# VectorE weights the expert activation and GpSimd makes the low part of the gated rows, in a DiT block's mixture of experts

## The chip, the cores and the metric
The kernel runs on one core of one Trainium2 chip. The metric is the device time of one execution in microseconds (us), given as the median of several runs. The engines are TensorE (PE, matmul), VectorE (DVE), ScalarE (ACT), GpSimd (POOL) and SyncE (SP, which issues most DMAs).

## The reference
The input is 16 batches of 512 rows of 128 numbers. Each batch goes through a modulated layer norm and routed linear attention, then through a second norm, a small gated layer and a mixture of experts. The part that matters here is the last one:

```python
g = _silu(jnp.einsum('td,edh->eth', xt, exp_w1))     # 8 experts
u = jnp.einsum('td,edh->eth', xt, exp_w3)
yexp = jnp.einsum('eth,ehd->etd', g * u, exp_w2)
routed = jnp.einsum('te,etd->td', combine, yexp)     # combine: the router's weights
shared = _silu(xt @ sh_w1) * (xt @ sh_w3) @ sh_w2    # two more "experts" of weight 1
```

The kernel puts the router's weight ahead of the last product: it multiplies the activation `g` by it, so that the ten products with `w2` can be summed in one PSUM bank.

## The kernel before
The program has three stages. In the first, all 16 batches are normalised and routed. The second runs the attention over 160 blocks. The third runs the experts over 160 units, one for each batch b and expert n (`k = 10*b + n`; n is 0 to 7 for the routed experts, and 8 and 9 for the two shared ones). Work that belongs to the batches and not to the loops (gather of the attended rows, projection, second norm, small gated layer, router) is cut into steps, the "post" jobs. `post_pool`, `post_act`, `post_pe`, `post_freed` and `post_dve` put each step into a fixed slot of the second and third loops, one batch every 10 slots. The last gather lies at unit 64 of the expert stage and the last router step at about unit 103, so the last 56 units have no such work.

Every engine runs its own instruction list in order, and the engines meet at semaphores. No scheduler changes the order: it is the order of the code. For one unit k the work is:

- PE, `up(k)`: three matmuls for the gate (bank 1 or 2) and three for the up part (one of three banks in `wide`). The operands are split into a high and a low part, so each product takes three passes (L1630).
- ACT: silu of the gate product into `eg` (named `kvw` in the trace, L1686).
- POOL: for n below 8, `eg` times the weight rows that a DMA has spread in `hq` (L1595).
- DVE: up part times `eg` into `ep` (also `kvw`, L1724).
- ACT: the high part of `ep`, a copy that rounds to the matmul's type, into `epp` (L1691).
- DVE: the low part, `ep` minus the high part (L1717).
- PE, `down(k)`: three matmuls with `w2`, summed over the batch in bank 0 (L1640). It is issued three units after `up(k)`.

`eg`, `ep` and `epp` are rings of three buffers. In its turn k, DVE runs freed and tail work, then the low part of unit k-1, then the product of unit k, then `post_dve`. ACT runs the tail, silu of unit k, the high part of unit k-1, then `post_act`. PE runs `up(k)`, `post_pe`, the tail of the batch before, then `down(k-3)`. POOL runs the weighting of unit k, a gather step in eight of ten units while gathers last (n = 7, 8, 9, 0 to 4, L898), and at n = 3 `hidden_parts`, which splits the rows of the batch after the next into high and low (L1547, L1549). The tail is the last gated layer: `ys`, the copy of bank 0 (L1672), two products (L1647, L1650), a transposition (L1654), and the vector and scalar steps between (L1701, L1678, L1707).

Post steps named below: L1048 to L1056 and L1140 (DVE, an inverse root in many tiny operations, at n = 1, 2, 3), L930 (ACT, the normalised rows, at n = 4), L957 (PE, transpositions, among others of L930's rows at n = 5 and of the gathered rows at n = 6), L909 (ACT, weights the gathered rows, at n = 5 and 6, and waits for the gathers), L936 (ACT, at n = 5, behind L909; the transposition at n = 6 waits for it), L1011 (PE, at n = 4, waits for the router's last step L1100 on DVE, once in four batches).

Of the kernel before, what the change touches and what calls it, by code (L numbers as in the profile page):

```python
# [5 lines left out]
ALU = mybir.AluOpType  # L6
# [8 lines left out]
P = 128  # L15
# [5 lines left out]
E = 8  # L21
# [31 lines left out]
def adaln_block(nc, x, gate_wT, q_w, k_w, v_wT, fmT, norm_c, o_wT, lin0, lin0_b, s1w1, s1b1, s1w2, s1b2, fgateT,  # L53
                ew1, ew3, ew2, shw1, shw3, shw2, lin1, lin1_b, s2w1, s2b1, s2w2, s2b2, cT, wmod, out):
    ctx = ExitStack()
    with ctx:
# [3 lines left out]
        def sem(name):  # L60
            return ctx.enter_context(nc.semaphore(name))
# [825 lines left out]
        def post_pool(pool, slot):  # L887
            for k in range(NT * TOPA):
                b = at(k - GATHER, slot)
                if b is not None:  # L890
                    u, s = b % 2, sum(b >= x for x in B0[1:])
                    if k == 0:
                        for i in range(2):
                            pool.wait_ge(s_os[i], 16 * ((C0[s + 1] // 2 + 1 - i) // 2))
                        if b >= 2:
                            pool.wait_ge(s_onT, b - 1)
                    t = b * NT + k // TOPA
                    pool.indirect_dma_start(gst[:, u, k, :], None, orow[s],  # L898
                                            bass.IndirectOffsetOnAxis(idxs[:, t, k % TOPA:k % TOPA + 1], 0),
                                            bounds_check=BLOCKS[s] * P - 1, oob_is_err=False).then_inc(s_g[u], 16)  # L900
# [258 lines left out]
        s_cb = [sem("weight_rows_loaded0"), sem("weight_rows_loaded1")]  # L1159

        def rows_of(u, lo, hi):
            return hq[:, (u * E + lo) * NT:(u * E + hi) * NT, 0:D]
# [10 lines left out]
        def tb(name, shape, dt=F32):  # L1173
            return ph.enter_context(nc.sbuf_tensor(name, shape, dt))
# [368 lines left out]
        def hidden_parts(pool, b, u):  # L1543
            pool.wait_ge(s_h2, b + 1)
            h = h_all[:, b * NT:(b + 1) * NT, :]
            high, low = (hp[:, u, k, :].rearrange("p (i d) -> p i d", d=D) for k in range(2))
            pool.tensor_copy(high, h)  # L1547
            pool.drain()  # L1548
            pool.tensor_tensor(low, h, high, ALU.subtract).then_inc(s_hl, 1)  # L1549

        RING = 3
        eg, ep = (kvw[:, i * RING * S:(i + 1) * RING * S].rearrange("p (r t) -> p r t", t=S) for i in range(2))
        epp = tb("epp", [P, RING, 2, S], F32R)
# [6 lines left out]
        UNITS = NB * NU  # L1560
# [6 lines left out]
        s_es = sem("expert_gate")  # L1567
        s_eu = sem("expert_gate_weighted")
        s_ep = sem("expert_hidden")
        s_eh = sem("expert_hidden_high")  # L1570
        s_el = sem("expert_hidden_low")
# [11 lines left out]
        with nc.Block() as block:  # L1583
            @block.gpsimd
            def _(pool):
                for b in range(2):
                    hidden_parts(pool, b, b)
                for k in range(UNITS):
                    b, n = divmod(k, NU)
                    if n < E:  # L1590
                        if n == 0:
                            pool.wait_ge(s_cb[b % 2], 16 * (b // 2 + 1))
                        pool.wait_ge(s_es, k + 1)
                        g = eg[:, k % RING, :].rearrange("p (i t) -> p i t", t=P)
                        pool.tensor_tensor(g, g, rows_of(b % 2, n, n + 1), ALU.mult).then_inc(s_eu, 1)  # L1595
                    post_pool(pool, NBK + k)
                    if n == 3 and 0 < b < NB - 1:
                        pool.wait_ge(s_eg, NU * b)
                        hidden_parts(pool, b + 1, (b + 1) % 2)
# [95 lines left out]
            @block.vector  # L1695
            def _(dve):
                def tail(b, n):
                    if n == T3 + 1:
                        dve.wait_ge(s_t3, b + 1)
                        dve.wait_ge(s_t2c, b + 1)  # L1700
                        dve.scalar_tensor_tensor(out=t2[:, :], in0=bank[7][:, :], scalar=bias[:, 5:6], in1=tg[:, :],  # L1701
                                                 op0=ALU.add, op1=ALU.mult).then_inc(s_t3c, 1)
                    elif n == T4 + 1:
                        dve.wait_ge(s_t5, b + 1)
                        if b >= 2:
                            dve.wait_ge(s_out[b % 2], 16 * (b // 2))
                        dve.tensor_tensor(fin[:, b % 2, :, :], bank[7][:, :].rearrange("p (i d) -> p i d", d=D),  # L1707
                                          x_all[:, b * NT:(b + 1) * NT, :], ALU.add).then_inc(s_fin, 1)

                for k in range(UNITS + NU):  # L1710
                    b, n = divmod(k, NU)
                    post_freed(dve, NBK + k)
                    if b:
                        tail(b - 1, n)
                    if 1 <= k <= UNITS:
                        dve.wait_ge(s_eh, k)
                        dve.tensor_tensor(epp[:, (k - 1) % RING, 1, :], ep[:, (k - 1) % RING, :],  # L1717
                                          epp[:, (k - 1) % RING, 0, :], ALU.subtract).then_inc(s_el, 1)
                    if b < NB:
                        if n < E:  # L1720
                            dve.wait_ge(s_eu, E * b + n + 1)
                        else:
                            dve.wait_ge(s_es, k + 1)
                        dve.tensor_tensor(ep[:, k % RING, :], up_bank[k % RING][:, :], eg[:, k % RING, :],  # L1724
                                          ALU.mult).then_inc(s_ep, 1)
                    post_dve(dve, NBK + k)
# [35 lines left out]
```

## Time and profile before
| | |
|---|---|
| median of 3 runs | 1312.92 us (1306.09 to 1319.36) |
| the profiled execution | 1298.82 us |
| its span, first to last instruction | 1297.1 us |
| PE, DVE, ACT, POOL busy | 84%, 72%, 52%, 38% |
| mean granted TensorE clock | 0.941 |

The span is split by the three stages: the expert stage has its first matmul at 769.5 us and its last work at 1294 us. A share of busy time averages over stages with different limits. The clock is a share of 2.4 GHz: 1.00 is 2.4 GHz, 0.50 is 1.2 GHz, and a value between says that both occurred.

### The profile page before, as it was taken

What the parts mean: (1) busy time and instruction counts of PE and PEld (TensorE: products, weight loads), DVE (VectorE), ACT (ScalarE), POOL (GpSimd) and SP (SyncE); (2) the same over time, 40 slices, a digit from 0 to 9 for tenths busy, and PEclk for the clock granted to TensorE, in tenths of its full rate; (3) what the DMA queues carried; (4) which work ended last, traced back from release to release, by engine and by line L of the source; (5) the groups of instructions that cost most, each with busy time, mean ns of one, the idle gap of its engine ahead of it and who ended that gap; (6) DMA issues with size and microseconds to landing.
All of it is one profiled execution on the core that took longest, in us unless ns stands there. A gap on an engine that the chain in (4) does not pass through costs nothing. (4 is left out here: it accounts for less than half of the span.)

```text
span 1297.1 us, 26776 instructions
## 1 busy us (share of the span) xinstructions
PE 1090.8 (84%) x9288; PEld 787.8 (61%) x9288; DVE 934.8 (72%) x2058; ACT 668.4 (52%) x1645; POOL 491.8 (38%) x450
## 2 busy tenths in 40 slices
PE   4875589999999887899988977778886799889996
PEld 3554456676676555566656645556664566667774
DVE  4774568788876665777778748787778887776664
ACT  2542245555555545556666535645555555445553
POOL 2057023313323544322211226656655433455542
PEclk8986689999999999999999989889888899999999
DMA  9962123323333333222222134123322023233220
GB/s 310 372 255 89 45 83 99 111 76 104 111 104 91 101 93 89 77 66 64 63 62 57 49 108 123 31 69 92 88 87 86 19 85 90 66 95 98 74 81 17
DMA packets 83586, 125.76 MB, mean 97 GB/s; under 512 B 9088, under 2 KB 65920, under 8 KB 79360
## 3 DMA queue, kind: packets, MB, share of 16 engines
q1 hardware_dynamic: 73216, 98.86, 25.0%
q0 software_dynamic: 10240, 25.18, 6.2%
q8 instruction: 79, 1.29, 0.4%
q14 instruction: 51, 0.42, 0.1%
HBM read 71.32 MB, written 52.69 MB: 96 GB/s over the span
## 5 line engine op out<-in xcount | busy, mean ns | idle before, releaser
L1486 DVE SCALAR_TENSOR_TENSOR att<-reach,endrel,wide 128x1024 f32<-128x1024 f32 x160 | 204.8, 1280 | 87.1 <-PE wide L1398 68.8
L1595 POOL TENSOR_TENSOR kvw<-kvw,hq 128x512 f32<-128x512 f32 x128 | 170.4, 1333 | 227.0 <-ACT kvw L1686 220.9
L898 POOL DMA_INDIRECT gst<-attended_rows,idxs x128 | 139.0, 1086 | 254.0 <-DVE att L1486 129.1
L1717 DVE TENSOR_TENSOR epp<-kvw,epp 128x512 fp32r<-128x512 f32 x160 | 153.8, 961 | 104.2 <-ACT epp L1691 102.1
L252 POOL DMA_INDIRECT routed_rows<-hq,idxs x128 | 132.0, 1031 | 224.6 <-DVE att L1486 150.3
L1640 PE MATMUL bank<-epp,w2p 128*128 128x512 f32 x480 | 172.2, 469 | 9.6 <-DVE epp L1717 9.4
L1686 ACT ACTIVATE kvw<-bank 128x512 f32<-128x512 f32 x160 | 94.5, 591 | 111.0 <-PE wide L1630 110.8
L1630 PE MATMUL bank<-hp,w1p 128*128 128x512 f32 x480 | 144.2, 410 | 5.7 <-POOL hp L1549 4.7
L1691 ACT ACTIVATE epp<-kvw 128x512 fp32r<-128x512 f32 x160 | 100.4, 628 | 92.3 <-DVE kvw L1724 92.1
L1373 PE MATMUL bank<-kvw,turned 128*128 x320 | 142.9, 529 | 5.5 <-ACT turned L1283 1.6
L1630 PE MATMUL wide<-hp,w3p 128*128 128x512 f32 x480 | 142.2, 406 | 0.0
L1640 PEld LDWEIGHTS bank<-epp,w2p 128*128 128x128 f32 x480 | 90.2, 197 | 54.9 <-issue 27.3
L1290 ACT ACTIVATE k1s<-bank 128x128 f32<-128x128 f32 x160 | 44.2, 276 | 150.5 <-PE bank L1373 142.5
L1398 PE MATMUL wide<-turned,kx 32*128 32x128 f32 x2560 | 117.7, 298 | 0.9 <-DVE att L1486 0.7
L1724 DVE TENSOR_TENSOR kvw<-wide,kvw 128x512 f32<-128x512 f32 x160 | 109.0, 681 | 10.4 <-POOL kvw L1595 10.4
L1630 PEld LDWEIGHTS bank<-hp,w1p 128*128 128x128 f32 x480 | 94.3, 197 | 31.0 <-POOL hp L1549 5.6
L1630 PEld LDWEIGHTS wide<-hp,w3p 128*128 128x128 f32 x480 | 93.3, 194 | 22.9
L1443 PE MATMUL bank<-att,vx 128*32 128x128 f32 x2560 | 103.9, 280 | 0.0
L1398 PEld LDWEIGHTS wide<-turned,kx 32*128 32x128 f32 x2560 | 87.3, 187 | 20.9 <-issue 2.4
L1479 DVE TENSOR_TENSOR hq<-bank,k1s 128x128 f32<-128x128 f32 x160 | 46.3, 289 | 47.6 <-ACT vx L1293 38.9
L1318 ACT ACTIVATE oTs<-bank 128x256 f32<-128x256 f32 x80 | 30.5, 381 | 95.1 <-PE bank L1443 63.5
L1435 PE MATMUL bank<-hq 128*128 128x128 f32 x320 | 66.2, 289 | 9.4 <-DVE sh L1496 9.1
(265 smaller groups left out, 1914.3 us busy)
## 6 DMA issues: line engine op xcount, KB each, us to landing
hq<-weight_rows SPq DMA_DIRECT2D x16, 2048.0 KB
routed_rows<-zero SPq DMA_DIRECT2D x4, 5120.0 KB, 24.5
rows<-routed_rows SPq DMA_DIRECT2D x80, 256.0 KB
attended_rows<-ob SPq DMA_DIRECT2D x80, 128.0 KB
out<-fin SPq DMA_DIRECT2D x16, 256.0 KB
routed_rows<-hq,idxs POOLq DMA_INDIRECT x128
gst<-attended_rows,idxs POOLq DMA_INDIRECT x128
hq<-in_ew SPq DMA_DIRECT2D x3, 512.0 KB, 6.7
```

The costliest lines, as they stand in the source:

```text
L252: pool.indirect_dma_start(hs[s], bass.IndirectOffsetOnAxis(idxs[:, t, k:k + 1], 0), hq[:, t, :], None, bounds_check=BLOCKS[s] * P - 1, oob ...
L898: pool.indirect_dma_start(gst[:, u, k, :], None, orow[s], bass.IndirectOffsetOnAxis(idxs[:, t, k % TOPA:k % TOPA + 1], 0), bounds_check=BL ...
L1373: pe.matmul(bank[1][:, 0:KV], turned[:, n // 2 % 3, 0, n % 2, :], kvw[:, bass.ds(w, KV)], start=True, stop=True).then_inc(s_kv, 1)
L1398: mm = pe.matmul(wide[:, p, par * P:(par + 1) * P], kx[r, n // 2 % 2, par, a * P:(a + 1) * P], turned[r, n // 2 % 3, 1, a, :], start=True, ...
L1443: mm = pe.matmul(bank[2][32 * p:32 * p + 32, n % 2 * P:(n % 2 + 1) * P], v[:, (4 * p + par) * DK:(4 * p + par + 2) * DK], att[:, n % 2, p, ...
L1486: dve.scalar_tensor_tensor(out=att[:, n % 2, :, :], in0=reach[:, :, :].rearrange("p a c -> p (a c)").unsqueeze(1) .to_broadcast([P, 4, 2 * ...
L1595: pool.tensor_tensor(g, g, rows_of(b % 2, n, n + 1), ALU.mult).then_inc(s_eu, 1)
L1630: mm = pe.matmul(ps[:, :], w[:, wk, n, :], hp[:, b % 2, hk, :], start=(wk + hk == 0), stop=(hk == 1))
L1640: mm = pe.matmul(bank[0][:, :], w2p[:, wk, n, :], epp[:, k % RING, hk, :], start=(n + wk + hk == 0), stop=(n == NU - 1 and hk == 1))
L1691: act.activation(epp[:, (k - 1) % RING, 0, :], ep[:, (k - 1) % RING, :], ACT.Copy).then_inc(s_eh, 1)
L1717: dve.tensor_tensor(epp[:, (k - 1) % RING, 1, :], ep[:, (k - 1) % RING, :], epp[:, (k - 1) % RING, 0, :], ALU.subtract).then_inc(s_el, 1)
L1724: dve.tensor_tensor(ep[:, k % RING, :], up_bank[k % RING][:, :], eg[:, k % RING, :], ALU.mult).then_inc(s_ep, 1)
```

## The change
The two SBUF operations of a unit change engines. The weighting of the activation goes from POOL to DVE, right ahead of the product with the up part. The low part goes from DVE to POOL. POOL's loop gets one more turn, since it now works on unit k-1. DVE's product gets a wait for the low part of unit k-3, because `ep` is now read by another engine than the one that writes it.

```diff
@@ gpsimd
-                for k in range(UNITS):
+                for k in range(UNITS + 1):
                     b, n = divmod(k, NU)
-                    if n < E:
-                        if n == 0:
-                            pool.wait_ge(s_cb[b % 2], 16 * (b // 2 + 1))
-                        pool.wait_ge(s_es, k + 1)
-                        g = eg[:, k % RING, :].rearrange("p (i t) -> p i t", t=P)
-                        pool.tensor_tensor(g, g, rows_of(b % 2, n, n + 1), ALU.mult).then_inc(s_eu, 1)
+                    if k:
+                        pool.wait_ge(s_eh, k)
+                        pool.tensor_tensor(epp[:, (k - 1) % RING, 1, :], ep[:, (k - 1) % RING, :],
+                                           epp[:, (k - 1) % RING, 0, :], ALU.subtract).then_inc(s_el, 1)
                     post_pool(pool, NBK + k)
@@ vector
                     if b:
                         tail(b - 1, n)
-                    if 1 <= k <= UNITS:
-                        dve.wait_ge(s_eh, k)
-                        dve.tensor_tensor(epp[:, (k - 1) % RING, 1, :], ep[:, (k - 1) % RING, :],
-                                          epp[:, (k - 1) % RING, 0, :], ALU.subtract).then_inc(s_el, 1)
                     if b < NB:
+                        dve.wait_ge(s_es, k + 1)
+                        if n == 0:
+                            dve.wait_ge(s_cb[b % 2], 16 * (b // 2 + 1))
                         if n < E:
+                            g = eg[:, k % RING, :].rearrange("p (i t) -> p i t", t=P)
+                            dve.tensor_tensor(g, g, rows_of(b % 2, n, n + 1), ALU.mult).then_inc(s_eu, 1)
                             dve.wait_ge(s_eu, E * b + n + 1)
-                        else:
-                            dve.wait_ge(s_es, k + 1)
+                        if k >= RING:
+                            dve.wait_ge(s_el, k - RING + 1)
                         dve.tensor_tensor(ep[:, k % RING, :], up_bank[k % RING][:, :], eg[:, k % RING, :],
                                           ALU.mult).then_inc(s_ep, 1)
```

The lines of the later part move up by one or two: the low part is L1592 (POOL), the weighting L1719 and the product L1723 (DVE).

VectorE, units 2 and 3 of the first batch, before; `expert_hidden_high` is ACT's rounded copy, `expert_gate_weighted` POOL's weighting, `deviation_chain` orders the tiny operations:

```order
L1053 SCALAR_TENSOR_TENSOR tmp<-tmp,var 128x36 [waits deviation_chain]
L1717 TENSOR_TENSOR epp<-kvw,epp 128x512 [waits expert_hidden_high,deviation_chain]
L1724 TENSOR_TENSOR kvw<-wide,kvw 128x512 [waits expert_gate_weighted]
L1056 SCALAR_TENSOR_TENSOR inv<-tmp,inv 128x36
L1051 TENSOR_TENSOR tmp<-inv 128x36 [waits deviation_chain]
```

The same place after the change; `expert_gate` is ACT's silu:

```order
L1053 SCALAR_TENSOR_TENSOR tmp<-tmp,var 128x36 [waits deviation_chain]
L1719 TENSOR_TENSOR kvw<-kvw,hq 128x512 [waits expert_gate,deviation_chain]
L1723 TENSOR_TENSOR kvw<-wide,kvw 128x512 [waits expert_gate_weighted]
L1056 SCALAR_TENSOR_TENSOR inv<-tmp,inv 128x36
L1051 TENSOR_TENSOR tmp<-inv 128x36 [waits deviation_chain]
```

The low part L1717, which waited for ACT's copy of the unit before, has left this list. Its place is taken by the weighting L1719, which waits for this unit's silu.

GpSimd, around `hidden_parts` of a batch with gathers, before (the three rows ahead of the cast are n = 2 and 3, the last two are n = 4):

```order
L898 DMA gst<-attended_rows3,idxs 128x128
L1595 TENSOR_TENSOR kvw<-kvw,hq 128x512 [waits expert_gate]
L898 DMA gst<-attended_rows3,idxs 128x128
L1547 CAST hp<-hq 128x512 [waits ff_hidden,expert_products]
L1549 TENSOR_TENSOR hp<-hq,hp 128x512
L1595 TENSOR_TENSOR kvw<-kvw,hq 128x512 [waits expert_gate]
L898 DMA gst<-attended_rows3,idxs 128x128
```

The same place after:

```order
L898 DMA gst<-attended_rows3,idxs 128x128
L1592 TENSOR_TENSOR epp<-kvw,epp 128x512 [waits expert_hidden_high]
L898 DMA gst<-attended_rows3,idxs 128x128
L1547 CAST hp<-hq 128x512 [waits ff_hidden,expert_products]
L1549 TENSOR_TENSOR hp<-hq,hp 128x512
L1592 TENSOR_TENSOR epp<-kvw,epp 128x512 [waits expert_hidden_high]
L898 DMA gst<-attended_rows3,idxs 128x128
```

The number of POOL operations between two gathers is the same here. What each waits for moved from the silu of unit k to the copy of unit k-1. At n = 8 and 9, where POOL had only the gathers, it now has a low part as well.

## Rows read from the trace of the kernel before
**Rows 1.** The page: the span, and TensorE's busy time, share and instructions.
```profile
span 1297.1 us, 26776 instructions
PE 1090.8 (84%) x9288; PEld 787.8 (61%) x9288; DVE 934.8 (72%) x2058; ACT 668.4 (52%) x1645; POOL 491.8 (38%) x450
```
**Rows 2.** Busy time by stretch: expert stage's start, gathers, other post work, rest.
```profile
core 0: us, PE busy (x) PEld busy (x) DVE busy (x) ACT busy (x) POOL busy (x), PEclk, DMA share, GB/s
766.00:800.00 34.00, 23.34 (x81) 16.37 (x82) 18.11 (x33) 13.45 (x29) 18.85 (x17) 0.85 0.47 137
800.00:1044.00 244.00, 196.86 (x799) 146.18 (x797) 192.56 (x377) 131.74 (x257) 134.79 (x110) 0.90 0.28 80
1044.00:1166.00 122.00, 108.21 (x452) 80.55 (x451) 96.12 (x165) 63.74 (x111) 51.28 (x41) 0.97 0.25 71
1166.00:1286.00 120.00, 114.88 (x478) 86.76 (x476) 78.85 (x110) 63.43 (x113) 61.71 (x47) 1.00 0.26 74
```
**Rows 3.** The page's costliest groups: the unit's two SBUF operations, ACT's copy, the product.
```profile
L1595 POOL TENSOR_TENSOR kvw<-kvw,hq 128x512 f32<-128x512 f32 x128 | 170.4, 1333 | 227.0 <-ACT kvw L1686 220.9
L1717 DVE TENSOR_TENSOR epp<-kvw,epp 128x512 fp32r<-128x512 f32 x160 | 153.8, 961 | 104.2 <-ACT epp L1691 102.1
L1691 ACT ACTIVATE epp<-kvw 128x512 fp32r<-128x512 f32 x160 | 100.4, 628 | 92.3 <-DVE kvw L1724 92.1
L1724 DVE TENSOR_TENSOR kvw<-wide,kvw 128x512 f32<-128x512 f32 x160 | 109.0, 681 | 10.4 <-POOL kvw L1595 10.4
```
**Rows 4.** TensorE's waits, 766 to 1044 us: in total, times, longest.
```profile
PE bank L957 <- ACT work L936: 24.2, 6, 7.3
PE bank L957 <- ACT work L930: 11.4, 5, 3.3
PE bank L1011 <- DVE wq L1100: 11.3, 2, 5.7
```
**Rows 5.** TensorE's waits, 1044 to 1166 us.
```profile
PE bank L957 <- ACT work L930: 5.9, 2, 3.1
PE bank L1640 <- DVE epp L1717: 3.5, 4, 1.3
```
**Rows 6.** TensorE's waits, from 1166 us to the end.
```profile
PE wide L1647 <- ACT ys L1672: 3.9, 6, 0.8
PE bank L1640 <- DVE epp L1717: 2.6, 3, 1.0
```
**Rows 7.** Timeline, one unit of the last batches: start us, us, engine, operation [idle before].
```profile
1213.53 0.69 DVE L1717 TENSOR_TENSOR epp<-kvw,epp 128x512 fp32r<-128x512 f32 x1 [0.70 <-ACT epp L1691]
1214.14 0.68 DVE L1724 TENSOR_TENSOR kvw<-wide,kvw 128x512 f32<-128x512 f32 x1
1214.86 0.63 ACT L1691 ACTIVATE epp<-kvw 128x512 fp32r<-128x512 f32 x1 [0.87 <-DVE kvw L1724]
...
1215.53 0.69 DVE L1717 TENSOR_TENSOR epp<-kvw,epp 128x512 fp32r<-128x512 f32 x1 [0.70 <-ACT epp L1691]
```
**Rows 8.** Timeline, a batch with gathers: the same columns.
```profile
896.72 1.77 DVE L1056 SCALAR_TENSOR_TENSOR inv<-tmp,inv 128x36 f32<-128x36 f32 x1
897.13 1.30 POOL L1595 TENSOR_TENSOR kvw<-kvw,hq 128x512 f32<-128x512 f32 x1
...
901.53 0.16 DVE L1140 SCALAR_TENSOR_TENSOR offset<-mv,inv 128x4 f32<-128x4 f32 x1
...
903.41 1.28 POOL L1595 TENSOR_TENSOR kvw<-kvw,hq 128x512 f32<-128x512 f32 x1
903.43 0.66 PE L957 MATMUL bank<-ident,work 128*128 128x128 f32 x4 [2.01 <-ACT work L930]
...
904.83 1.05 POOL L898 DMA_INDIRECT gst<-attended_rows,idxs  x1
...
908.33 1.26 ACT L909 ACTIVATE gst<-gst,wslot 128x128 f32<-128x128 f32 x4
...
910.40 1.08 PE L957 MATMUL bank<-ident,gst 128*128 128x128 f32 x4 [4.21 <-ACT work L936]
```

## The prediction
> **What bounds the kernel now.** I read the page first. TensorE is busy 84% of the span [rows 1], but that is a mean over three stages, and the change touches only the last one. So next comes the table by stretch [rows 2]. The reader is to see four stretches. In the last (1166 to 1286 us) TensorE is busy 114.88 of 120 us at full clock: it is the bound, and no other engine can give back more than 5 us there. In the stretch with gathers (800 to 1044 us) it is busy 196.86 of 244 us, at a clock of 0.90. Between them (1044 to 1166 us) it is busy 108.21 of 122 us at 0.97. So room lies in TensorE's idle time and in the time at the low clock, and both are largest where the post jobs are.
>
> Then the costliest groups [rows 3]. Two of them wait for each other: the low part L1717 was idle 102.1 us for ACT's copy L1691, and that copy was idle 92.1 us for DVE's product L1724. The timeline shows why [rows 7]: low part 1213.53, product 1214.14, copy 1214.86, next low part 1215.53. DVE's list has the low part of unit k-1 ahead of the product of unit k, so product, copy and low part form a closed loop of 2.00 us a unit. TensorE's nine matmuls of a unit take 9 x 0.233 = 2.1 us here (an estimate from the stretch's 120 us for 478 matmuls, 0.251 each, less the tails' share). The loop is just below that when nothing disturbs it. It is disturbed often: the low part takes 961 ns in the mean of 160 [rows 3] and 0.69 in the clean rows [rows 7], so 160 x 0.27 = 43 us of DVE time are stretch. Last, the waits of TensorE itself [rows 4 to 6], since only those can become time.
>
> **What moves, and at what price.** DVE gives up 160 low parts and gets 128 weightings, also of two SBUF inputs of the same size. I take the clean 0.69 for both [rows 7], so DVE loses 32 x 0.69 = 22 us of work. The bounds for a weighting are 0.69 and the mean 0.96 of the low part. The product now waits for the weighting on its own engine, and no longer starts 0.61 after the row ahead of it as in rows 7. I put 0.1 on that, 128 x 0.1 = 13 us. DVE is busy 78.85 of 120 us in the last stretch [rows 2], so this is covered there. POOL gives up 128 operations of 1.33 and gets 160 of the same form, +32 x 1.33 = 43 us. In the last two stretches it is busy about half of the time or less [rows 2], so that is covered too. In the gather stretch it isn't fully covered, see below.
>
> The loop of rows 7 opens. DVE no longer waits for ACT's copy. A unit's way from silu to `down` is now weighting 0.69, product 0.68, copy 0.63, low part 1.3: 3.3 us, and before it was 1.3, 0.68, 0.63, 0.69, the same 3.3 us. `down` comes three units (6.3 us or more) behind `up`, so the longer last link is covered. DVE's new wait for the low part of unit k-3 is met by the same margin. Behind it on DVE stand the product and all post steps.
>
> **The sum, by TensorE's idle rows.**
>
> *From 1166 us to the end* [rows 6]. The six waits for `ys` (3.9 us) come from ACT standing at its copy for the late product. With the loop open the copy follows the silu at once, and I take all 3.9. The three waits for the low part (2.6 us) lie at the very end, after the last `up`. There the product is earlier, but the last two low parts take 1.3 and not 0.69. I take 1 of 2.6. Together 4.9 us; bounds 0 and 6.5.
>
> *1044 to 1166 us* [rows 5]. Two waits for L930 (5.9 us) come from DVE being late with the tiny operations L1048 to L1140. One of these took 1.77 us because POOL's weighting ran beside it: it started at 896.72, the weighting ended at 898.43 [rows 8]. Such an operation takes about 0.2 when alone, as L1140 with 0.16 shows. After the change it still meets a POOL operation, which now starts after ACT's copy and not after the silu, so part of this lateness stays. I take 3.5 of 5.9. The four waits for the low part (3.5 us) are replaced by POOL's, which have more slack outside the router's steps: 3 of 3.5. The clock of 0.97 over 122 us means 7.3 us at 1.2 GHz. TensorE stood idle before it, and a shorter idle time may keep it away: 1.8 us, half of what it costs. Together 8.3 us; bounds 0 and 13.
>
> *766 to 1044 us* [rows 4]. The largest wait is 24.2 us for L936. The reader should follow rows 8: POOL starts a weighting at 903.41 and the gather at 904.83 to 905.88, and only then can L909 (908.33) run, with L936 and the transposition of 910.40 behind it. This chain goes through POOL's list, and that is as full as before: one operation of 1.3 and one gather of 1.05 to 1.3 in each unit, and `hidden_parts` at n = 3. So L909 can start at most 908.33 - 905.88 = 2.45 us earlier a batch (less what the gather takes to land, which no row shows), and POOL's work itself starts about 0.5 later (one copy of 0.63 behind the silu). In plain batches I take 0 for L936 and also 0 for the 11.4 us for L930: the time gained there is lost again one unit later at the gathers. In the two batches whose wait for L936 is 7.3 (the router's step stands in the way there), I take the difference to the plain 4.2, less a little: 2 x 2.5 = 5 us. L1011's 11.3 us wait for DVE, which is less loaded: 4 us. Smaller stalls for the low part at the start: 1.5. Together 10.5 us; bounds -10 (POOL's list 1.5 us a batch longer) and +35 (L930's, L1011's and half of L936's waits).
>
> The sum is 4.9 + 8.3 + 10.5 = 23.7, so **24 us**. Against the profiled execution's 1298.82 us that is 1275. That execution was 14 us faster than the median of the runs shown. I take the same 24 us from the median 1312.92: **1289 us**, 1.8% faster.
>
> **The port that DVE and GpSimd share.** Rows 8 show a tiny DVE operation that ended 0.06 after POOL's. The Trainium skill, in "SBUF — State Buffer", section "SBUF: two separate sides", says that a DVE operation with two SBUF inputs and a GpSimd operation exclude each other for the whole instruction, and that a PSUM operand avoids it. This trace agrees as far as the product goes, 681 ns in the mean of 160 beside POOL's work [rows 3]. The rule speaks against the change, since both moved operations have two SBUF inputs and POOL's number grows; it is the mechanism of the second rival.
>
> **Rivals.** *1. The gains are handed back at the gathers and in the router's steps.* Only the last stretch and half of the middle one pay: 4.9 + 4 = 9 us, 1304. For it: POOL's chain in rows 8, and DVE busy 192.56 of 244 us. Against it: part of DVE's lateness comes from waiting for copies [rows 3].
>
> *2. Slower: the weighting and POOL's low part block each other while POOL is full.* In the gather stretch POOL's turn is 1.3 plus gather 1.05 to 1.3 plus gaps, near the 2.9 us that TensorE takes with a post job. If each low part must also wait for a whole weighting (0.69), that is 57 gathers' units x 0.69 = 39 us, all on the chain that ends at L909. Less the 8 us that the last two stretches would still give, it is +31, 1344. The point from which it decides is 24 / 57 = 0.4 us more a unit: there the gain is gone. Against it: the weighting starts right at the silu's end, one copy (0.63) before the low part can start, so that it is mostly over by then. If DVE is late, this order is lost.
>
> *3. The change does little:* TensorE is the bound in the last stretch, and in the others another post job is late next. Then the time is 1313. The program does do what it says, so this needs equal stalls in new places.
>
> *4. More than forecast:* L930's waits go in the gather stretch as well, and the low clock with them: another 20 us, 1269.
>
> **Chances.** Forecast, 12 to 40 us less, with the fourth case 0.62. First rival with the third 0.22. Second rival 0.16, of which a part is within 1%. About 1% (13 us) is what a measurement of this kernel can tell from no change. So faster by over 1% is 0.62, within 1% 0.23, slower 0.15. The range reaches from the fourth case, 1270, to a quarter of the second rival's loss, 1320. Nearly 1 in 10 lies beyond each end.
>
> **What the profile after would show.** Right: the group of the weighting on DVE with a mean under 0.85; ACT's copy hardly idle for the product; no wait of L1647 for `ys`; TensorE's idle for L930 between 1044 and 1166 us down to 2 or 3 us; the wait for L936 still there, and no smaller in plain batches. Wrong: a weighting mean near 1.3 (the port decides), POOL's turn in the gather stretch above 3.3 us, or a new wait of TensorE's L1638 (`down`) for POOL's low part, above all after `hidden_parts`. The prediction would also be wrong if TensorE's longer idle ahead of the gathers' transposition put more of the stretch at 1.2 GHz than the 0.90 of now.

## The result, and the profile after
The changed kernel takes 1296.45 us in the median of four runs (1293.75 to 1300.29), beside 1309.51 for the kernel before (four runs, 1305.64 to 1319.36). The medians lie 13 us apart. The ratio is 0.989, with a 95% interval of 0.984 to 0.994: 14 us less (8 to 21), where 24 were forecast. The profiled execution took 1293.75 us.

The page of the changed kernel, its span and its busy times; after it the groups that answer to [rows 3]:

```profile
span 1292.0 us, 26928 instructions
PE 1090.2 (84%) x9288; PEld 787.8 (61%) x9288; DVE 910.7 (70%) x2026; ACT 668.4 (52%) x1645; POOL 532.3 (41%) x482
...
L1592 POOL TENSOR_TENSOR epp<-kvw,epp 128x512 fp32r<-128x512 f32 x160 | 215.9, 1350 | 183.7 <-ACT epp L1689 183.1
L1719 DVE TENSOR_TENSOR kvw<-kvw,hq 128x512 f32<-128x512 f32 x128 | 113.6, 888 | 94.1 <-ACT kvw L1684 90.6
L1723 DVE TENSOR_TENSOR kvw<-wide,kvw 128x512 f32<-128x512 f32 x160 | 110.5, 691 | 27.1 <-ACT kvw L1684 22.6
L1689 ACT ACTIVATE epp<-kvw 128x512 fp32r<-128x512 f32 x160 | 100.2, 626 | 48.0 <-DVE kvw L1723 44.4
```

TensorE does the same work in the same time as before. ACT's copy L1689 was idle 44.4 us for the product, and before it was 92.1 [rows 3]. The weighting on DVE took 888 ns in the mean, a little over the 0.85 that the prediction had set as its mark, and well below 1.3. The table by stretch, with the columns of [rows 2]:

```profile
766.00:800.00 34.00, 20.59 (x69) 13.70 (x69) 16.99 (x37) 11.10 (x24) 17.04 (x14) 0.85 0.48 137
800.00:1044.00 244.00, 197.84 (x805) 146.74 (x806) 185.74 (x363) 135.26 (x266) 153.53 (x125) 0.92 0.28 79
1044.00:1166.00 122.00, 109.86 (x455) 80.95 (x454) 90.48 (x159) 62.97 (x111) 62.53 (x49) 0.97 0.26 73
1166.00:1286.00 120.00, 116.94 (x488) 89.08 (x486) 71.14 (x99) 65.00 (x116) 74.92 (x59) 1.00 0.26 74
```

The expert stage began 4.3 us later in this execution (773.83 against 769.49 us), so these stretches hold slightly earlier work than those of before. I therefore also cut the stage by batches, each from the product of its unit 0 to that of the next batch. The stage took 515.8 us, and before 525.2: 9.4 less. Another run of the changed kernel (below) gave 514.5. By batches, in us (b11 to b14 are the full-rate batches, with no post jobs; b15 runs to the end):

```
              b0   b1   b2   b3   b4   b5   b6   b7   b8   b9   b10  b11 to b14  b15
before        32.1 42.3 37.4 36.9 37.2 42.2 37.3 32.7 29.2 34.0 26.1 24.3, 24.2  32.1
after         32.3 38.6 39.4 37.3 37.8 38.4 39.8 32.0 30.7 30.1 26.6 23.1 each   31.9
```

Now TensorE's waits after, as in [rows 4 to 6]: 766 to 1044 us, then 1044 to 1166, then from 1166 us to the end.

```profile
PE bank L957 <- ACT work L936: 23.3, 7, 6.3
PE bank L957 <- ACT work L930: 12.1, 5, 4.1
PE bank L1011 <- DVE wq L1100: 11.9, 2, 6.0
...
PE wide L1645 <- ACT ys L1670: 3.5, 4, 1.5
```
```profile
PE bank L957 <- ACT work L930: 4.7, 2, 2.5
PE wide L1645 <- ACT ys L1670: 3.3, 3, 2.8
PE bank L1638 <- POOL epp L1592: 0.9, 3, 0.4
```
```profile
PE bank L1638 <- POOL epp L1592: 1.4, 2, 1.1
...
PE wide L1645 <- ACT ys L1670: 0.7, 1, 0.7
```

The three large waits of the gather stretch stand as before. In the last stretch the wait for `ys` fell from 3.9 to 0.7 us. The timeline of a unit there, as in [rows 7], shows the new order:

```profile
1212.16 0.60 ACT L1684 ACTIVATE kvw<-bank 128x512 f32<-128x512 f32 x1 [0.98 <-PE wide L1628]
1212.65 0.62 ACT L1689 ACTIVATE epp<-kvw 128x512 fp32r<-128x512 f32 x1
1212.79 0.69 DVE L1719 TENSOR_TENSOR kvw<-kvw,hq 128x512 f32<-128x512 f32 x1 [0.68 <-ACT kvw L1684]
1213.36 1.29 POOL L1592 TENSOR_TENSOR epp<-kvw,epp 128x512 fp32r<-128x512 f32 x1 [0.80 <-ACT epp L1689]
1213.52 0.69 DVE L1723 TENSOR_TENSOR kvw<-wide,kvw 128x512 f32<-128x512 f32 x1
...
1214.89 0.69 DVE L1719 TENSOR_TENSOR kvw<-kvw,hq 128x512 f32<-128x512 f32 x1 [0.68 <-ACT kvw L1684]
```

ACT's copy starts right behind the silu, which waited for TensorE and for nothing else. Between two weightings lie 2.10 us here, and 2.00 lay between the low parts of [rows 7]; but ten units took 24.2 us there and take 23.1 now. Of these 1.1 us, 0.75 are TensorE's wait for `ys`, which batches b12 to b15 had before and no longer have; the rest was not traced. The same batch as in [rows 8], with gathers:

```profile
890.98 1.51 DVE L1719 TENSOR_TENSOR kvw<-kvw,hq 128x512 f32<-128x512 f32 x1
...
893.97 0.69 DVE L1719 TENSOR_TENSOR kvw<-kvw,hq 128x512 f32<-128x512 f32 x1
893.97 1.85 POOL L1592 TENSOR_TENSOR epp<-kvw,epp 128x512 fp32r<-128x512 f32 x1 [0.58 <-ACT epp L1689]
...
898.45 1.02 POOL L898 DMA_INDIRECT gst<-attended_rows,idxs  x1 [0.16 <-issue]
898.85 2.00 DVE L1056 SCALAR_TENSOR_TENSOR inv<-tmp,inv 128x36 f32<-128x36 f32 x1
899.50 1.28 POOL L1592 TENSOR_TENSOR epp<-kvw,epp 128x512 fp32r<-128x512 f32 x1
...
907.67 1.03 POOL L898 DMA_INDIRECT gst<-attended_rows,idxs  x1
...
910.32 1.28 ACT L909 ACTIVATE gst<-gst,wslot 128x128 f32<-128x128 f32 x4 [1.53 <-DMA gst<-attended_rows,idxs]
```

L909 waits for the gather to land. It starts 1.6 us after GpSimd's record of the gather ends (908.70). The two operations that start together at 893.97 show the port that DVE and GpSimd share: DVE's takes its clean 0.69, and POOL's takes 1.85 in place of 1.29. At 898.85 it is the other way about: a small DVE operation, which starts beside the gather, ends at 900.85, 0.07 after the low part behind that gather.

### The profile page after: what moved, and what is told of

The parts are those of the page before. It is cut to its first block and busy times, and to the rows that moved or that the text cites. A ratio compares the mean times of both kernels' runs of the same rounds, so it can differ in the third digit from the quotient of the medians.

```text
span 1292.0 us, 26928 instructions
## 1 busy us (share of the span) xinstructions
PE 1090.2 (84%) x9288; PEld 787.8 (61%) x9288; DVE 910.7 (70%) x2026; ACT 668.4 (52%) x1645; POOL 532.3 (41%) x482
## 3 DMA queue, kind: packets, MB, share of 16 engines
q8 instruction: 79, 1.29, 0.4%
## 5 line engine op out<-in xcount | busy, mean ns | idle before, releaser
L1592 POOL TENSOR_TENSOR epp<-kvw,epp 128x512 fp32r<-128x512 f32 x160 | 215.9, 1350 | 183.7 <-ACT epp L1689 183.1
L1486 DVE SCALAR_TENSOR_TENSOR att<-reach,endrel,wide 128x1024 f32<-128x1024 f32 x160 | 204.8, 1280 | 87.8 <-PE wide L1398 65.2
L1719 DVE TENSOR_TENSOR kvw<-kvw,hq 128x512 f32<-128x512 f32 x128 | 113.6, 888 | 94.1 <-ACT kvw L1684 90.6
L1723 DVE TENSOR_TENSOR kvw<-wide,kvw 128x512 f32<-128x512 f32 x160 | 110.5, 691 | 27.1 <-ACT kvw L1684 22.6
L1689 ACT ACTIVATE epp<-kvw 128x512 fp32r<-128x512 f32 x160 | 100.2, 626 | 48.0 <-DVE kvw L1723 44.4
L1398 PE MATMUL wide<-turned,kx 32*128 32x128 f32 x2560 | 119.2, 301 | 0.8 <-DVE att L1486 0.4
L1628 PEld LDWEIGHTS bank<-hp,w1p 128*128 128x128 f32 x480 | 93.3, 196 | 34.4 <-POOL hp L1549 7.0
L1398 PEld LDWEIGHTS wide<-turned,kx 32*128 32x128 f32 x2560 | 88.6, 190 | 21.1 <-issue 3.0
```

The lines of the kernel that those rows point to most:

```text
L1398: mm = pe.matmul(wide[:, p, par * P:(par + 1) * P], kx[r, n // 2 % 2, par, a * P:(a + 1) * P], turned[r, n // 2 % 3, 1, a, :], start=True, ...
L1486: dve.scalar_tensor_tensor(out=att[:, n % 2, :, :], in0=reach[:, :, :].rearrange("p a c -> p (a c)").unsqueeze(1) .to_broadcast([P, 4, 2 * ...
L1592: pool.tensor_tensor(epp[:, (k - 1) % RING, 1, :], ep[:, (k - 1) % RING, :], epp[:, (k - 1) % RING, 0, :], ALU.subtract).then_inc(s_el, 1)
L1628: mm = pe.matmul(ps[:, :], w[:, wk, n, :], hp[:, b % 2, hk, :], start=(wk + hk == 0), stop=(hk == 1))
L1689: act.activation(epp[:, (k - 1) % RING, 0, :], ep[:, (k - 1) % RING, :], ACT.Copy).then_inc(s_eh, 1)
L1719: dve.tensor_tensor(g, g, rows_of(b % 2, n, n + 1), ALU.mult).then_inc(s_eu, 1)
```

## The experiments
Runs 1 to 4 shared one chip (kernel before: 1310.75 us), and runs 5 to 12 another (1237.52 us beside 5 to 8, 1240.3 beside 9 to 12). So only ratios to the kernel before on the same chip are compared, and beside them the length of the expert stage, which is alike on both. Ratios stand with their 95% intervals. The diffs are shortened: the waits that belong to a moved line move with it and are not all shown, and a name like "low part of unit k-1" stands for its lines.

**1. The order alone.** The prediction's mechanism was that the loop of product, copy and low part opens. This opens it without a change of engines:

```diff
@@ before, vector
-  low part of unit k-1
   (weighted activation waited for)
+  if k >= RING: dve.wait_ge(s_el, k - RING + 1)
   product of unit k
+  low part of unit k-1
```

> The kernel before with one thing moved: DVE makes the low part of unit k-1 behind the product of unit k instead of ahead of it. The weighting stays on GpSimd, the low part on DVE. Theory A (the gain of the change is the opened loop product, copy, low part, and an order on DVE opens it as well): the batches from 1166 us on take 23.1 us as in the changed kernel and not 24.2, the wait of TensorE for ys (3.9 us there) goes, and the time is 8 to 14 us below the kernel before, 0.990 to 0.994. Theory B (the gain is that the two operations changed engines, and GpSimd's load moved behind the product): nothing changes, 24.2 us a batch, ratio 0.998 to 1.002.

Measured: a ratio of 1.001 (0.9975 to 1.0045), 1309.92 us. The stage took 530.5 us, and a full-rate batch 25.5 where before had 24.2. The largest groups and a piece of the timeline:

```profile
L1722 DVE TENSOR_TENSOR kvw<-wide,kvw 128x512 f32<-128x512 f32 x160 | 110.2, 689 | 127.4 <-POOL kvw L1595 121.8 <-ACT kvw L1686 4.2
```
```profile
1226.37 1.73 POOL L1549 TENSOR_TENSOR hp<-hq,hp 128x512 fp32r<-128x512 f32 x1
...
1228.07 1.29 POOL L1595 TENSOR_TENSOR kvw<-kvw,hq 128x512 f32<-128x512 f32 x1
1229.39 0.69 DVE L1722 TENSOR_TENSOR kvw<-wide,kvw 128x512 f32<-128x512 f32 x1 [2.44 <-POOL kvw L1595]
```

DVE's wait for ACT's copy is gone, and its product now waits 121.8 us for POOL's weighting (before: 10.4 [rows 3]). The loop was only what ended last. Right behind it stood POOL's weighting between silu and product. In plain turns of a full-rate batch that costs nothing (2.1 us a unit, as in the changed kernel). The loss lies behind `hidden_parts`, as in the rows above: the product waits 2.44 us for the weighting that GpSimd makes late, and the turn after it takes 4.6 us, where the changed kernel takes 3.35. So theory B holds for the time, but not for the batches, which got 1.3 us longer.

**2. `hidden_parts` at n = 5.** It leaves POOL's list ahead of the last gathers of a batch:

```diff
@@ after, gpsimd
-                    if n == 3 and 0 < b < NB - 1:
+                    if n == 5 and 0 < b < NB - 1:
```

> The changed kernel with hidden_parts at n = 5 instead of n = 3, so that the low part and the gather of n = 4 no longer stand behind it on GpSimd. Theory A (in the gather stretch GpSimd's list up to the last gather decides when L909 and L936 run, and TensorE waits for them): the last gather of a batch comes some 3.5 us earlier, TensorE's 23.3 us of waits for L936 fall to 5 or less, batches 2 to 4 take 33 to 35 us instead of 37 to 39, and the time is 15 to 25 us below the changed kernel, 0.972 to 0.98 of the kernel before. Theory B (DVE's lateness with the tiny operations and the router's steps decides): the wait for L936 changes into one for L930 or L919 and the time stays within 3 us of the changed kernel, 0.988 to 0.992.

Measured: 0.980 (0.977 to 0.982), where the change itself has 0.989. Plain batches b3 and b4 took 33.6 and 34.4 us and had 37.3 and 37.8. TensorE's waits, 766 to 1044 us:

```profile
PE bank L957 <- ACT work L936: 18.9, 7, 6.1
...
PE bank L1011 <- DVE wq L1100: 10.8, 2, 5.4
```

The wait for L936 in plain batches went from 4.3 to 2.3 us. This shows that POOL's list holds the chain there. Theory A had the sum of these waits at 5 us or less, and 18.9 stayed: 12.1 of them lie in b1 and b5, the batches with the router's steps (6.1 each, 6.3 before the edit), which POOL's list hardly holds. A full-rate batch paid a little (23.9 us, 23.1 before the edit).

**3. The gathers' consumers one unit later:**

```diff
@@ after, post_act: weighting of the gathered rows (L909), squares
-                b = at(half - 11, slot)
+                b = at(half - 10, slot)
-            b = at(-8, slot)
+            b = at(-7, slot)
@@ after, post_dve: sum and reduction of them
-            b = at(-9, slot)
+            b = at(-8, slot)
-            b = at(-7, slot)
+            b = at(-6, slot)
```

> The changed kernel with the users of the gathered rows one unit later: L909 at n = 6 and 7, the sum at n = 8, the squares at n = 9, the reduction at n = 0. GpSimd's list is as it was. Theory A (L936 and the silu of n = 5 stand behind L909, which waits for the last gather): the wait for L936 goes nearly whole, 15 to 25 us less than the changed kernel, 0.972 to 0.98 of the kernel before. Theory B (TensorE would wait for something else at n = 6 to 8 anyway): at most 3 us less.

Measured: 0.985 (0.981 to 0.989), the stage 505.7 us. TensorE's waits, 766 to 1044 us:

```profile
PE bank L957 <- ACT work L936: 11.0, 4, 4.2
...
PE wide L1645 <- ACT ys L1670: 6.8, 6, 2.0
```

12 us of L936's waits went, and 3 us came back at `ys`. The gain is 5 us, between the two theories.

**4. A weighting without the port.** ACT leaves the silu of a routed unit in its PSUM bank, and DVE's weighting reads it there. TensorE's next gate product waits for the weighting too:

```diff
@@ after, tensor
                         pe.wait_ge(s_es, k - 1)
+                        if (k - 2) % NU < E:
+                            pe.wait_ge(s_eu, E * ((k - 2) // NU) + (k - 2) % NU + 1)
@@ scalar
-                        act.activation(eg[:, k % RING, :], gate_bank[k % 2][:, :], ACT.Silu).then_inc(s_es, 1)
+                        act.activation(gate_bank[k % 2][:, :] if n < E else eg[:, k % RING, :], gate_bank[k % 2][:, :],
+                                       ACT.Silu).then_inc(s_es, 1)
@@ vector
-                            dve.tensor_tensor(g, g, rows_of(b % 2, n, n + 1), ALU.mult).then_inc(s_eu, 1)
+                            dve.tensor_tensor(g, gate_bank[k % 2][:, :].rearrange("p (i t) -> p i t", t=P),
+                                              rows_of(b % 2, n, n + 1), ALU.mult).then_inc(s_eu, 1)
```

> The changed kernel, with the silu of the routed units written in place in its PSUM bank, so that the weighting on DVE reads one PSUM and one SBUF operand. TensorE's gate bank comes free after the weighting and not after the silu. It tests what it costs that weighting and low part have two SBUF inputs each. Theory A (they block each other, and this is felt): the weighting's mean falls from 888 ns to about 690, the low part on GpSimd from 1350 to 1300, and the time by 5 to 12 us below the changed kernel. Theory B (they block each other, but other work covers it): the same means, and the time within 3 us of the changed kernel. Theory C (no blocking, the long ones are something else): the mean stays above 800 ns.

Measured: 0.976 (0.973 to 0.979), 1279.59 us, 17 us below the change. The stage took 493.0 us. The page's groups, then TensorE's waits from 766 to 1044 us:

```profile
L1592 POOL TENSOR_TENSOR epp<-kvw,epp 128x512 fp32r<-128x512 f32 x160 | 207.1, 1294 | 175.2 <-ACT epp L1692 174.6
L1722 DVE TENSOR_TENSOR kvw<-bank,hq 128x512 f32<-128x512 f32 x128 | 88.4, 691 | 100.8 <-ACT bank L1686 97.8 <-DMA hq<-weight_rows 1.9
```
```profile
PE bank L957 <- ACT work L936: 27.8, 7, 7.3
...
PE bank L957 <- ACT work L930: 1.4, 1, 1.4
```

Both moved operations lost their stretch (888 to 691 ns and 1350 to 1294 ns), and the wait for L930 in this stretch fell from 12.1 to 1.4 us. So the cost of the weighting's conflict was real and lay on the path. Other conflicts stayed: the post jobs L1109 and L1147, also of two SBUF inputs, took 1.04 and 1.05 us from 766 to 1166 us, and 1.08 and 1.03 in the changed kernel.

The Trainium skill, "SBUF — State Buffer", section "SBUF: two separate sides", says that a VectorE operation with at most one SBUF input, outside the modes that use two ports, doesn't contend with GpSimd. The 691 ns agree. It says that whoever starts first blocks the other for the whole instruction. The 0.69 beside 1.85 us of the changed kernel agree. The small operation of 2.00 us began beside a gather and ended with the low part behind it: it didn't get in between the two.

**5 and 10. Weighting to DVE, low part stays on DVE.** This is the first half of the change; GpSimd keeps only gathers and `hidden_parts`:

```diff
@@ before, gpsimd
-                        pool.tensor_tensor(g, g, rows_of(b % 2, n, n + 1), ALU.mult).then_inc(s_eu, 1)
+                    if k:
+                        pool.wait_ge(s_eu, E * b + min(n, E))
@@ before, vector, ahead of the low part of unit k-1
+                            dve.tensor_tensor(g, g, rows_of(b % 2, n, n + 1), ALU.mult).then_inc(s_eu, 1)
```

> One half of the change alone: the weighting moves to DVE, and the low part stays there too, in the order weighting of unit k, low part of unit k-1, product of unit k. GpSimd keeps only gathers and hidden_parts. Theory A (GpSimd's two-input operation in the chain and at the port is what costs; DVE has room): the weighting hides ACT's copy, no stretch is left on DVE, a full-rate batch takes 23 to 24 us, and with DVE busy 236 of 244 us in the gather stretch the time comes out near the changed kernel, 0.985 to 0.995 of the kernel before. Theory B (the loop product, copy, low part bounds the unit): the loop is back at 0.69 + 0.63 + 0.69, with a weighting beside the copy, 2.1 us or more a unit, batches of 24.5 us or more, and DVE's load makes the stretch with post jobs longer: slower than the changed kernel by 10 to 30 us.

Measured: 0.980 (0.973 to 0.986), the stage 499.4 us. That is better than either theory, and the half alone is better than the whole. Since this decides the account, it was run again beside the change itself:

> The half change once more: weighting and low part both on DVE. Theory A (moving the low part to GpSimd costs): 0.975 to 0.985 and the expert stage 10 to 20 us shorter than the changed kernel's. Theory B (the difference lay between the chips): within 4 us of the changed kernel.

Measured: 0.979 (0.975 to 0.982), the stage 499.9 us. Its groups:

```profile
L1720 DVE TENSOR_TENSOR epp<-kvw,epp 128x512 fp32r<-128x512 f32 x160 | 115.0, 719 | 21.7 <-ACT epp L1687 18.9
L1717 DVE TENSOR_TENSOR kvw<-kvw,hq 128x512 f32<-128x512 f32 x128 | 90.8, 709 | 50.9 <-ACT kvw L1682 46.4 <-DMA hq<-weight_rows 2.6
```

Without a GpSimd neighbour both DVE operations are near 0.7 us. DVE does all of this work, and a full-rate batch still takes 23.3 us.

**9. The change again, on this chip:**

> The changed kernel itself, on one chip with the two runs below, because the half change e5 was faster (0.980 of the kernel before, on another chip) than the whole (0.989). If that order is real, this one comes out 0.985 to 0.993, and its expert stage (first matmul to the end) takes some 516 us. If it was the chip, it comes out near 0.980.

Measured: 0.991 (0.987 to 0.994), the stage 514.5 us. It lies above run 10 by 1.2%, and the intervals don't touch. The batches say where. In the full-rate batches the two are alike (23.1 and 23.3 us). In plain batches with gathers run 10 takes 32.2 and 33.8 us (b3, b4) where the changed kernel takes 36.9 and 37.1, and TensorE's wait for L936 there is 2.3 us in place of 4.1 to 4.3, as in run 2. So a good part of the low part's price on GpSimd is paid in GpSimd's list ahead of the gathers.

**11. Low part to GpSimd, weighting stays there ahead of it.** This is the second half alone:

```diff
@@ before, gpsimd, behind the weighting of unit k
+                    if k:
+                        pool.wait_ge(s_eh, k)
+                        pool.tensor_tensor(epp[:, (k - 1) % RING, 1, :], ep[:, (k - 1) % RING, :],
+                                           epp[:, (k - 1) % RING, 0, :], ALU.subtract).then_inc(s_el, 1)
@@ before, vector
-  low part of unit k-1
+                        if k >= RING:
+                            dve.wait_ge(s_el, k - RING + 1)
```

> The other half alone: the low part moves to GpSimd, and the weighting stays there, ahead of it. GpSimd then has two operations of 1.3 us a unit, 2.75 us with their gaps, where TensorE needs 2.1. So GpSimd bounds the last stretch: 8 x 2.75 + 2 x 1.4 + hidden_parts 2.6 = 27 to 28 us a batch instead of 24.2, and with gathers 1.3 more in eight units of ten, 38 to 42 us a batch. Time 30 to 60 us above the kernel before, 1.025 to 1.045. If it came out below the kernel before, the low part's place on GpSimd would be a gain by itself.

Measured: 1.035 (1.030 to 1.040), the stage 570.1 us. Its groups, and GpSimd's timeline:

```profile
L1726 DVE TENSOR_TENSOR kvw<-wide,kvw 128x512 f32<-128x512 f32 x160 | 110.0, 690 | 245.5 <-POOL kvw L1595 232.1 <-ACT kvw L1690 12.2 <-DVE choice L1090 0.3
```
```profile
1150.07 1.29 POOL L1598 TENSOR_TENSOR epp<-kvw,epp 128x512 fp32r<-128x512 f32 x1
...
1151.32 1.30 POOL L1595 TENSOR_TENSOR kvw<-kvw,hq 128x512 f32<-128x512 f32 x1
```

Two operations of 1.3 us a unit fill GpSimd, and the product waits for it. A full-rate batch takes 26.7 us. The four corners, as ratios: neither move 1, weighting alone 0.979, low part alone 1.035, both 0.991. The moves are not additive, but in either row the low part on GpSimd costs something: 1.2% with the weighting gone from there, 3.5% with it present.

**6. `hidden_parts` at n = 5 in the kernel before.** The edit of run 2, made to the other kernel:

> The kernel before (not the changed one) with hidden_parts at n = 5. It tells whether the 13 us that this gave on the changed kernel need the change. Theory A (GpSimd's list up to the last gather bounds the gather stretch in both kernels): the same 10 to 15 us, 0.989 to 0.992. Theory B (before, the weighting of n = 4 behind hidden_parts held up the product and so DVE's whole list, and the change had taken that away already): more than that, 18 to 25 us, 0.981 to 0.986.

Measured: 0.9955 (0.992 to 0.999). Both theories had a larger gain. Plain batches gained here too (33.2 and 34.1 us for b3 and b4, before 36.9 and 37.2), but full-rate batches rose from 24.2 to 25.7 us; in run 2 the same edit took them from 23.1 to 23.9. A late weighting on GpSimd delays the product, and a late low part is felt less. So part of what the change is worth shows only together with this edit: with `hidden_parts` at n = 5 in both kernels it is 0.980 / 0.9955 = 0.984 (an estimate across the two chips), and 0.989 without.

**7. Runs 4, 2 and 3 together:**

> The changed kernel with the three edits together: weighting from PSUM, hidden_parts at n = 5, users of the gathered rows one unit later. If the waits for L936 (27.8 us with the first edit alone) come from GpSimd's chain, they fall below 6 us now, because the last gather is 3.5 us earlier and its use one unit later. Theory A (the stalls are in series, and the edits add up): 1279.6 less 12 to 20 us, 1260 to 1268, ratio 0.962 to 0.968. Theory B (one stall takes the place of the other, the router's L1011 and ys): 1272 to 1278.

Measured: 0.958 (0.953 to 0.963), the stage 475.1 us. The three gains apart would add up to 0.962.

**8. And the router's steps one unit earlier:**

```diff
@@ run 7, post_dve
-                r = group(part, slot)
+                r = group(part - 1, slot)
```

> The kernel of the three edits together, and the router's steps on DVE one unit earlier, while TensorE's transposition L1011 stays at its unit. Theory A (L1011 waits because DVE's chain of router steps ends just too late): the two waits of 4.3 us fall by one unit's time, to 1.5 or less each, and the time by 4 to 8 us below the three edits together. Theory B (the router's steps only add load on DVE, wherever they stand): within 2 us.

Measured: 0.954 (0.950 to 0.959), 1182.81 us, the stage 470.5 us. TensorE's waits in the gather stretch (700 to 984 us), first of run 7, then of run 8:

```profile
PE bank L957 <- ACT work L936: 10.4, 5, 3.9
PE bank L1011 <- DVE wq L1100: 10.3, 2, 5.2
```
```profile
PE bank L957 <- ACT work L936: 12.9, 5, 5.1
```

The waits for the router's last step fell from 10.3 to 1.1 us in two places. Batches b2 and b6 gained 5.9 and 6.7 us (37.7 and 38.5 to 31.8), and b1 and b5 gave back 4.0 and 4.2 (34.4 and 34.1 to 38.4 and 38.3).

**12. Everything on DVE, with the three moves of slots of run 8:**

> Weighting and low part on DVE, with the three moves of slots of e8: hidden_parts at n = 5, users of the gathered rows one unit later, the router's steps one unit earlier. e8 has the low part on GpSimd and the weighting from PSUM, 0.954. Theory A (with GpSimd's chain and the port out of the way DVE's load now bounds the stretch with post jobs): 31 to 33 us for a plain batch with gathers, and slower than e8, 0.958 to 0.968. Theory B (DVE has room enough): as fast as e8 or faster, 0.945 to 0.955.

Measured: 0.965 (0.962 to 0.969), the stage 480.8 us. With the same slots, run 8 has the low part on GpSimd and the weighting from PSUM, and is 1.1% better. So with the weighting read from PSUM the low part may well stand on GpSimd; which of the two differences carries the 1.1% was not separated.

## Why the prediction was right, and where not
The sign and the range held. Of the 24 us forecast, 13 to 14 came (12 by the ratio of run 9), at the lower edge of the forecast's own 12 to 40. The stage in the traces got 9.4 us shorter; the rest of the 14 isn't in these two traces, and single executions of one kernel differ by as much. By stretch (cut by batches):

| | forecast | measured in the stage |
|---|---|---|
| last stretch (b11 to end) | -4.9 | -4.6 |
| middle (b7 to b10) | -8.3 | -2.6 |
| gathers (b0 to b6) | -10.5 | -2.0 |

**The last stretch** was right in size. The waits for `ys` went from 3.9 to 0.7 us, and the low part's from 2.6 to 1.4 [rows 6], where 3.9 and 1 had been taken.

**The plain batches of the gather stretch** were right: 0 was taken for them, and b3 and b4 took 0.4 and 0.6 us more. The wait for L936 in b3 is 4.36 us after 4.21. The reason given was right as well: L909 waits for the gather, and runs 2 and 3, which loosen just that, gain where the change does not.

**The terms for the router failed.** "L1011's 11.3 us wait for DVE, which is less loaded: 4 us" measured -0.6: the wait rose to 11.9. The lighter load didn't reach the operation that L1011 waits for. The router's last step L1100 reads two SBUF operands, and from 766 to 1166 us it stretched, first before, then after:

```profile
L1100 DVE TENSOR_TENSOR wq<-choice,top 128x128 f32<-128x128 f32 x3 | 1.4, 452 | 0.1
```
```profile
L1100 DVE TENSOR_TENSOR wq<-choice,top 128x128 f32<-128x128 f32 x3 | 4.0, 1340 | 0.1
```

In run 4 it takes 475 ns, and the wait is 8.6. The larger part of the wait hangs on the slots in which the router's steps stand: run 8, which moves these by one unit, brings it down to 1.1.

"2 x 2.5 = 5 us" for L936 in b1 and b5 measured 1.9: the waits went from 7.3 to 6.3 each. These batches did gain 3.8 us each, but 1.75 of that in each is a wait that the sum had not named, of the router's first product L1003 for L1024, DVE's last step of the small gated layer. Before, from 766 to 1044 us, it stood in the list of TensorE's waits, and after it is gone:

```profile
PE bank L1003 <- DVE hq L1024: 3.5, 2, 1.8
```

That gain was luck. Batches b2 and b6 gave back 2.0 and 2.4 us, partly in new waits for `ys`, 1.48 us in each. The 1.5 us for the start did not come either (b0 +0.2): of the low part's 3.3 us of waits there 2.4 went, and L930 and L936 took 0.8 more each.

**The middle stretch** was over-sized. Of its terms, 1.2 of the 3.5 us for L930 came [rows 5], and 2.6 of the 3 for the low part. The 1.8 us of clock did not come: the granted clock is 0.97 again. The wait for `ys` in b10 rose from 1.9 to 2.8 us, and b8 even grew by 1.4 us while its waits shrank, at a granted clock of 0.94 (1076 to 1107 us) where before it was 1.00 (1076 to 1105).

**In the stage, the first rival's sum came nearer than the forecast's.** It had the gains handed back at the gathers and in the router's steps, and 9 us left: 4.9 in the last stretch and 4 in the middle. The stage measured 9.4, with 4.6, 2.6 and 2.0 in the three stretches, and b2 and b6 handed back 4.4 us of what b1 and b5 gained. The medians of whole executions (13 us) lie between that rival's 9 and the forecast's 24.

**The port** was under-priced in the forecast's own terms. The weighting was taken at 0.69 and took 0.888 us, 25 us more of DVE's time in all, and other DVE operations with two SBUF inputs stretched as well: the router's L1100 above, and the post jobs of the gathered rows. In the groups of DVE from 766 to 1166 us, L1109 and L1147 had 676 and 682 ns before, and now:

```profile
L1147 DVE TENSOR_TENSOR gst<-gst,inv 128x512 f32<-128x512 f32 x8 | 8.2, 1026 | 0.0
L1109 DVE TENSOR_TENSOR gst<-gst 128x512 f32<-128x512 f32 x7 | 7.5, 1078 | 0.0
```

Not all of them did: the small operations L1056 and L1053 fell from 773 to 661 and from 441 to 261 ns.

Run 4 puts a price on it: 17 us for taking the conflict out of the weighting, while L1109 and L1147 kept theirs. That is the second rival's mechanism. It had been priced at 39 us (57 units with gathers, where the trace has 53) on a chain where it hardly acts (run 4's wait for L936 is 27.8 us, no lower), and it acted at L930 and L1011 instead, through DVE being late. So 14 us may stand for a gain of about 31 less a port of 17. That last sum is argued from run 4 and not shown apart, since run 4 also changes when TensorE may start the next gate product.

**The mechanism was half right.** "The loop opens" describes the trace, but run 1 opens it and gains nothing. What the change is worth comes from GpSimd's 1.3 us leaving the way from silu to product, where VectorE's 0.69 takes its place: runs 5 and 10 do that without the second move and get 0.979. The full-rate batches show it with no gathers in the way: 25.5 us with the order alone, 23.3 with the weighting on VectorE. In the batches with gathers runs 5 and 10 gain by GpSimd's shorter list as well (L936's wait of 4.2 us in a plain batch becomes 2.3), and how much of the 2.1% is which was not separated. The prediction counted both ways as "the same 3.3 us" from silu to `down`, and asked only for the end of the chain. The reason, as runs 1 and 11 show it in the product's waits of 121.8 and 232.1 us: the early links hold DVE, and behind the product ACT's copy, each with a list of other work behind it, and the last link holds only TensorE's `down`, three units behind, which waited 3.2 us in all for GpSimd's low part in the changed kernel. The second move, the low part to GpSimd, cost 1.2% as made, most visibly at the gathers.

## What to carry to other kernels
In a chain over several in-order engines, if the slow engine must have a step, try it last, where the consumer is several units behind, and not early, where its lateness stands in front of all that the faster engines do next; the length of the whole chain doesn't tell this. Count what else stands in the slow engine's list: here its gathers came later for it. When a change moves two operations, run each move alone: here one was worth 2.1% and the other cost 1.2%. Check a forecast stretch by stretch, since a total can be met by a gain that nobody named. Where VectorE and GpSimd both read two SBUF operands, try leaving one operand in PSUM before moving work between them.

## What the runs showed that was not expected
The kernel before took 1310.75 us on one chip and 1237.5 to 1240.3 on another, 5.5% less, while the changed kernel's expert stage was 515.8 and 514.5 us long. Most of the difference lies in the stage ahead, the attention (in the traces of the changed kernel its line L1486 runs from 171.4 to 763.9 us on the first chip and from 161.4 to 700.0 on the second; the operation takes 1281 ns on both, and DVE's idle time ahead of it for TensorE's L1398 is 65.2 us and 35.3). TensorE is busy 534 and 519 us there, at a granted clock of 0.98 and 1.00, so most of the 54 us is idle time. No experiment here looked into that, and the cause stays open. An absolute time of one chip can't be set beside one of the other.

A VectorE operation can also be held for longer than one compute instruction of GpSimd's: a weighting of 0.69 us took up to 2.51 us in the changed kernel, and one of the 0.2 us operations L1056 took 2.00 in the batch shown, with gathers and low parts alternating on GpSimd. The same holds for the 1.77 us of the kernel before [rows 8], which the prediction put down to the weighting beside it. The operation started at 896.72, 0.41 us ahead of that weighting, and so beside the gather in front of it (895.57 to 897.11 in that trace). Which phase of the gather blocks such an operation was not tried.
